# Router logits of an attention and expert block as four column-tiled products, with the expert choice moved later

## The reference

```
mod = silu(c) @ wmod                      # shifts, scales and gates a batch
h = layernorm(x) * (1 + ca) + sa
q = h @ W + b
w = exp(tanh((q @ h.T) * 1/|i - j|)), 0 on the diagonal
x = x + ga * (w @ h) / sum(w)
h2 = layernorm(x) * (1 + cb) + sb
logits = h2 @ Wg                          # 8 experts a token
top 2 of the 8, softmax over the two
x = x + gb * (sum over the two of weight * expert(h2) + shared(h2))
expert(h) = relu(h @ W1 + b1) @ W2 + b2, 128 -> 512 -> 128
```

## Time and profile before

| | us |
|---|---|
| median of 3 runs | 650.99 (649.42 to 651.34) |
| profiled execution, first to last instruction (its span) | 665.5 |
| TensorE busy in it | 618.6 (93%) |
| VectorE busy | 457.9 (69%) |
| ScalarE busy | 397.5 (60%) |
| POOL busy | 343.3 (52%) |

### The profile page before, as it was taken

The page is one execution under the profiler, slowest core; times in us unless marked ns, Lnnn a source line. Parts: engine busy times, 40 slices in busy tenths (PEclk is TensorE's granted clock), DMA queues, the critical chain, the costliest instruction groups (busy, mean ns, idle before and its releaser), DMA issues.

```text
span 665.5 us, 13395 instructions
## 1 busy us (share of the span) xinstructions
PE 618.6 (93%) x4311; PEld 560.6 (84%) x4311; DVE 457.9 (69%) x1415; ACT 397.5 (60%) x635; POOL 343.3 (52%) x341
## 2 busy tenths in 40 slices
PE   3898999999999998977898999999999999999995
PEld 3587988898889886866798999998989898898995
DVE  7889797989898969766666564544444454452698
ACT  3587887877878756524346556565555646463541
POOL 4541706757575765657460465655565656465100
PEclk9899999999999999887999999999999999999998
DMA  8030000111111111111165466656666665521692
GB/s 299 27 158 1 1 1 17 37 34 33 34 33 38 33 42 33 37 39 43 49 196 200 129 197 190 181 172 193 195 188 182 187 182 178 175 65 30 268 386 113
DMA packets 29884, 76.44 MB, mean 115 GB/s; under 512 B 7126, under 2 KB 11374, under 8 KB 29712
## 3 DMA queue, kind: packets, MB, share of 16 engines
q1 hardware_dynamic: 20480, 58.49, 27.2%
q0 software_dynamic: 8640, 16.93, 7.5%
q10 hardware_dynamic: 720, 0.47, 0.2%
HBM read 53.53 MB, written 23.24 MB: 115 GB/s over the span
## 4 chain that ended last, share of the span: by engine, by line
PE 33%; DVE 8%; issue 5%; another core or an unknown queue 2%; DMA 2%; POOL 2%; ACT 1%; SPq 0%; POOLq 0%; ACTq 0%; DVEq 0%
PE value L1940 12%; PE score L1733 5%; PE misc L1940 5%; PE score L1731 5%; PE score L1732 4%; PE value L1991 2%; POOL rows_x L576 2%; DVE h_hi L1271 1%; DMA h_t<-rows_z 1%; ACT work L967 1%; DVE tile_y L1560 1%; PE misc L1772 1%; DVE tile_y L1552 0%; DMA lw<-rows_x 0%
## 5 line engine op out<-in xcount | busy, mean ns | idle before, releaser
L780 POOL DMA_INDIRECT rows_z<-tile_y,tags x138 | 142.5, 1032 | 118.8 <-issue 37.5
L1731 PE MATMUL score<-h_hi,h_lo 128*128 128x512 f32 (+1 forms) x252 | 94.9, 376 | 3.9 <-DVE rows_all L1177 3.8
L1759 PE MATMUL value<-w_ring,work 128*128 128x129 f32 x768 | 93.8, 279 | 1.6 <-ACT work L840 1.0
L1759 PEld LDWEIGHTS value<-w_ring,work 128*128 128x128 f32 x768 | 91.2, 194 | 4.1 <-issue 1.6
L967 ACT ACTIVATE work<-score,w_ring 128x512 f32<-128x512 f32 (+1 forms) x96 | 53.2, 616 | 61.7 <-PE score L1733 44.5
L1733 PE MATMUL score<-h_hi,h_lo 128*128 128x512 f32 (+1 forms) x252 | 89.4, 355 | 0.0
L1732 PE MATMUL score<-h_hi,h_lo 128*128 128x512 f32 (+1 forms) x252 | 88.9, 353 | 0.0
L576 POOL DMA_INDIRECT rows_x<-work,slot x64 | 64.5, 1008 | 45.5 <-issue 16.3
L838 ACT ACTIVATE work<-work 128x1024 f32<-128x1024 f32 x64 | 67.2, 1050 | 27.2 <-DVE work L1168 22.1
L1168 DVE TENSOR_TENSOR work<-score,lw 128x1024 f32<-128x1024 f32 x64 | 76.6, 1216 | 2.7 <-PE score L1733 1.2
L967 ACT ACTIVATE work<-score,w_shared 128x512 f32<-128x512 f32 x64 | 39.9, 685 | 57.9 <-PE score L1733 45.6
(11 more groups left out here) (254 smaller groups left out, 1269.0 us busy)
## 6 DMA issues: line engine op xcount, KB each, us to landing
w_ring<-packs SPq DMA_DIRECT2D x24, 578.0 KB
rows_all<-packs SPq DMA_DIRECT2D x23, 578.0 KB
lw<-rows_x SPq DMA_DIRECT2D x24, 260.0 KB
res<-x SPq DMA_DIRECT2D x8, 512.0 KB, 6.3
h_t<-rows_z SPq DMA_DIRECT2D x3, 1024.0 KB, 11.0
mod<-mod_rows SPq DMA_DIRECT2D x1, 2560.0 KB, 10.1
rows_z<-tile_y,tags POOLq DMA_INDIRECT x142
rows_all<-rows_z SPq DMA_DIRECT2D x2, 1024.0 KB, 13.0
```

The costliest lines, as they stand in the source:

```text
L780: nc.gpsimd.indirect_dma_start(rows_z[:, :], bass.IndirectOffsetOnAxis(ap=tags[pos][:, k, 0:1].bitcast(I32), axis=0), tile_y[par][:, k, :] ...
L1731: nc.tensor.matmul(out, a_lo, b_hi, start=True, stop=False)
L1759: ins = nc.tensor.matmul(value[:, s // 3, c0:c0 + D + 1], prob[:, t % 4, s * P:(s + 1) * P], normal[b % 3][:, t, :], start=(t == 0 and s % ...
```

## The change

The weights of the router are padded from 8 to 32 columns with zeros, and the roles are swapped: they become the stationary side, and 256 tokens the moving side. Four such products (`gate_panes`) fill `misc`: pane j takes tokens 256j to 256j + 255 of the batch's order and writes partitions 32j to 32j + 31, that is, column tile j of TensorE's array. ScalarE copies the 128x256 result to `gate_t` (`stage_gate`), TensorE transposes it back in two pieces (`gate_logits`), and VectorE's `choose` copies the 8 of each 32 columns that count. In batches 2 to 7 the transposes, the choice and the count of batch b - 2 now stand in batch b instead of at the end of batch b - 1. `take_ranks` moves behind `scale_attended`, `ranks` behind `scores(b, 2)`.

```diff
-        wg_sb = sb("wg_sb", [D, E])
+        wg_sb = sb("wg_sb", [D, COL])
+        gate_t = sb("gate_t", [P, S // PANES])
...
+            nc.gpsimd.memset(wg_sb[:, E:COL], 0.0).then_inc(wg_cleared, 1)
             nc.gpsimd.iota(lw_from[:, :].rearrange("p (g q) -> p g q", q=P), pattern=[[1, G], [G, P]],
...
+            def stage_gate(b):
+                act.wait_ge(gate_ps_ready, b + 1)
+                nc.scalar.activation(gate_t[:, :], misc[:, 0:S // PANES], ACT.Copy).then_inc(gate_staged, 1)
...
             def last_batch(b):
-                gap_exponent(b - 2)
+                stage_gate(b - 2)
                 weights(b, 0)
                 weights(b, 1)
+                gap_exponent(b - 2)
...
                 weights(b, 6)
+                stage_gate(b - 1)
                 weights(b, 7)
...
                     return last_batch(b)
+                stage_gate(b - 2)
                 transposed(b + 1, 1 - par, 0)
...
             stage_h2t(B - 1, 1, xt_ps)
+            stage_gate(B - 1)
             split_x(3, 1, shared_rows(3))
...
-                nc.vector.tensor_copy(logits[:, :, :].rearrange("p g e -> p (g e)"), misc[:, 0:G * E]).then_inc(logits_ready, 1)
+                gates = misc[:, S // PANES:2 * (S // PANES)].rearrange("p (t j e) -> p t j e", j=PANES, e=COL)
+                nc.vector.tensor_copy(logits[:, :, :].rearrange("p (j t) e -> p t j e", j=PANES), gates[:, :, :, 0:E]).then_inc(logits_ready, 1)
...
-                if exists(b - 2):
-                    count_chosen(b - 2, route_chain[b - 2])
                 weigh(b, 0)
+                route_chain[b - 2] = choose(b - 2)
                 weigh(b, 1)
+                count_chosen(b - 2, route_chain[b - 2])
                 attend(b - 1)
-                if exists(b - 2):
-                    take_ranks(b - 2)
                 scale_attended(b - 1)
+                take_ranks(b - 2)
                 weigh(b, 2)
...
-                route_chain[b - 1] = choose(b - 1)
...
+            def gate_panes(b):
+                pe.wait_ge(h2t_staged, 2 * b + 2)
+                if b == 0:
+                    pe.wait_ge(wg_cleared, 1)
+                for j in range(PANES):
+                    at = b * S + j * (S // PANES)
+                    ins = nc.tensor.matmul(misc[j * COL:(j + 1) * COL, 0:S // PANES], wg_sb[:, :], h2_t[:, at:at + S // PANES], start=True, stop=True)
+                ins.then_inc(gate_ps_ready, 1)
+
             def gate_logits(b):
-                pe.wait_ge(h2t_staged, 2 * b + 2)
-                for g in range(G):
-                    ins = nc.tensor.matmul(misc[:, g * E:(g + 1) * E], h2_t[:, b * S + g * P:b * S + (g + 1) * P], wg_sb[:, :], start=True, stop=True)
+                pe.wait_ge(gate_staged, b + 1)
+                for t in range(S // PANES // P):
+                    ins = nc.tensor.transpose(misc[:, S // PANES + t * P:S // PANES + (t + 1) * P], gate_t[:, t * P:(t + 1) * P], ident[:, :])
                 ins.then_inc(logits_ps_ready, 1)
...
                 scores(b, par, 0)
+                gate_logits(b - 2)
                 scores(b, par, 1)
                 pe.wait_ge(qt_ready, 2 * b + 2)
                 transpose_h(b + 1, 0)
                 values(b - 1, 1 - par, 6)
                 values(b - 1, 1 - par, 7)
-                if exists(b - 2):
-                    pe.wait_ge(ht_ready, 2 * b + 3)
-                    ranks(b - 2)
                 scores(b, par, 2)
+                pe.wait_ge(ht_ready, 2 * b + 3)
+                ranks(b - 2)
                 transpose_h(b + 1, 1)
...
-                gate_logits(b - 1)
+                gate_panes(b - 1)
...
             transpose_h2(B - 1, 1, xt_ps, last_xhat)
+            gate_panes(B - 1)
             gate_logits(B - 1)
```

More of the change, by code:

```diff
@@ L61 @@
 FRONT = 8
+PANES = 4
+COL = P // PANES
 RING = 3
@@ L310, in adaln_moe @@
         h2t_staged = sem("h2t_staged")
+        wg_cleared = sem("wg_cleared")
+        gate_ps_ready = sem("gate_ps_ready")
+        gate_staged = sem("gate_staged")
         logits_ps_ready = sem("logits_ps_ready")
@@ L803, in _ @@
             act.dma_start(batt_sb[:, :], b_att).then_inc(small_loaded, 16)
-            act.dma_start(wg_sb[:, :], wg).then_inc(small_loaded, 16)
+            act.dma_start(wg_sb[:, 0:E], wg).then_inc(small_loaded, 16)
             def modulation():
@@ L1310, in last_batch @@
             def last_batch(b):
+                weigh(b, 0)
+                route_chain[b - 2] = choose(b - 2)
+                attend(b - 1)
+                weigh(b, 1)
                 count_chosen(b - 2, route_chain[b - 2])
-                weigh(b, 0)
-                attend(b - 1)
+                weigh(b, 2)
                 take_ranks(b - 2)
-                weigh(b, 1)
-                weigh(b, 2)
                 weigh(b, 3)
@@ L1805, in last_batch @@
                 scores(b, par, 0)
+                gate_logits(b - 2)
                 values(b - 1, 1 - par, 7)
                 scores(b, par, 1)
+                scores(b, par, 2)
                 ranks(b - 2)
-                scores(b, par, 2)
                 scores(b, par, 3)
```

## The result

The changed kernel takes **686.76 us** (median of 6 runs, 684.90 to 691.48), the kernel before 651.16 beside it: ratio 1.055, 95% interval 1.053 to 1.057, so +35.6 us. The profiled execution of the change is itself the longest of its six: its mean granted clock is 0.953, that of the other five 0.960 to 0.970, so it holds more of the clock's loss than the median does. That of the kernel before, shown above, is 14.5 us over its median.

The account below looks back on a forecast made before the run. It took TensorE to bound batches 2 to 6. Stops and added work +24 us, clock +7, batch 7 +0.5, last logits +0.8 and memset +0.2 made +32.5, carried to the 651 us median: 683 us, range 665 to 695.

Parts of the forecast that it names:

- The wait for ScalarE: TensorE, before the gate transposes in batches 2 to 6: stands still 2.5 us for ScalarE's queued copy.
- the rival's 3.8: Same place, if the panes run side by side: TensorE stands still 3.8 us, transposes starting at the same time.
- The wait for the ranks: TensorE, before transpose_h(b + 1, 1): stops 2.8 us until VectorE's later take_ranks, where there was 0.3.
- The clock: Behind the ten new stops in batches 2 to 6: half are followed by low clock, +7 us (0 to +17).
- VectorE's order: VectorE in the batches: the choice moved later frees it where it only waited, 0 us.
- The sum of five batches: Batches 2 to 6: +24 us from +4.8 per batch, plus 7 for the clock.
- Batch 7: Batch 7: no stop for ScalarE, ranks wait for a later count; 0 to +1, taken as +0.5 us.
- The last logits: End of the attention stage: +0.8 us with panes one after the other, or -1.5 side by side.
- panes side by side: Rival: TensorE saves 1.0 us per batch, gaining only in batch 7 and the tail; 680 us, chance 0.15.
- Only one stop costs: Rival: ScalarE's lag shrinks, so the first stop goes and the second stays; 666 us, chance 0.10.
- Faster: Rival: copy finds ScalarE free (lag under 3.2 us), ranks read in time, panes parallel; 640 us, chance 0.05.

Follow-up runs that it names:

- e1: The changed kernel with ScalarE's copy of the panes moved ahead of weights(b, 6): 676.0 us, 1.038 of the kernel before.
- The fillers: The run e4: dummy products that nothing waits for keep TensorE busy in both stops of the changed kernel; 678.2 us.
- e4: The changed kernel with dummy products filling TensorE's two stops, nothing waiting for them: 678.2 us, 1.042 of the kernel before.
- e3: The changed kernel with both edits, the copy ahead of weights(b, 6) and take_ranks directly behind attend: 664.1 us, 1.022 of the kernel before.
- the second trace of before: The kernel before, unchanged, profiled once more: span 649.4 us, batches 2 to 6 in 160.6 us.
- e7: The kernel of e6 with four more panes a batch, all eight's extra four written to one column tile: 662.1 us, 1.017 of the kernel before.
- e5: The changed kernel's new order with the eight products of before, no copy and no transposes: 680.4 us, 1.046 of the kernel before.
- e6: The changed kernel's panes, copy and transposes with, as near as possible, the order of before on every engine: 649.9 us, 0.9992 of the kernel before.
- e2: The changed kernel with take_ranks back directly behind attend, ahead of scale_attended: 673.2 us, 1.034 of the kernel before.
- e11: The same text as e6, run again on another chip: 678.3 us, 1.016 of the kernel before, which took 667.0 us there.

## Why the prediction was right, and where it was off

683 us was forecast, 686.8 measured. Step by step, from one batch's logits to the query product of the next (batch 3):

| stretch | before (first trace) | forecast | measured |
|---|---|---|---|
| logits to gate transposes | - | 5.74 | 5.80 |
| to the scores behind the values | - | 5.65 | 7.20 |
| to `transpose_h(b + 1, 1)` | - | 4.55 | 4.59 |
| to the query product | - | 3.8 | 6.47 |
| together | 14.94 | 19.7 | 24.06 |

- **The wait for ScalarE** ended where it was forecast (panes + 5.74), since ScalarE's queue sets it. Its length was 3.56 us, not 2.5: the panes run side by side, so TensorE arrives earlier, which the prediction had as the rival's 3.8 at the same end. In batch 2 it was 2.80. The copy took 0.37 (taken 0.45).
- **The wait for the ranks:** 2.62 us, five times (taken 2.8), and the old 0.50 us at the query product is gone, both as the text had it. In e1 it grew to 3.49 us when the choice moved ahead.
- **The clock** is the mis-sized term: "If half of ten fall", 1.7 us each, taken as +7. Nine of ten fell. The table holds 1.6 us of slow rows behind the first stop and 2.7 behind the second; by the same rows it is 2.6, 4.2, 4.3, 2.7 and 4.1 us in batches 2 to 6, together 18 us. The fillers gave back 12 us of them between the traces and 8.5 us in the plain runs, whose clock was higher than the traced one's. So half of the falls had been left out, and two things that the sum did not have worked against that: a part of the first fall lies under VectorE's chain, and some of the time comes back as other waits. By the plain runs +7 was near.
- **VectorE's order** was put at nothing ("The choice moved later frees VectorE at a place where it only waited: 0"). With a full clock, in e4, the way from the gate transposes to the second stop's end took 10.1, 11.6, 11.0, 10.7 and 10.7 us, where the forecast had 10.2: choice and count now stand between `weigh(b, 0)` and `attend`, and in e1 and e3 the ranks wait 1.8 to 1.95 us for the count in batches 3 to 6.
- **The sum of five batches** was 24 + 7; measured 39.7, and 27.3 with the fillers. **Batch 7**, taken +0.5, measured +2.6: the ranks wait 2.65 us for the later count there, where the second trace of before has 0.23, and the clock falls behind that wait (0.50 from 293.5 to 297.5 us); I had put the wait at 1 at most, without following VectorE's order.
- **The last logits**, taken +0.8 (serial) or -1.5 (side by side), measured 2.76 us to VectorE's read instead of 3.62, -0.86: the panes are side by side (1.08 us at the low clock), but VectorE read the logits 0.5 us late, behind its own residual work. All that follows the last logits' start is 1.3 us shorter, so nothing of it was lost.
- **The nearness of the number is in part luck:** +32 was forecast, the plain runs have +35.6 and the traces +40.3. The five batches were 8.7 us too low and batch 7 2.1, the last logits and what follows were too high, and the plain runs have a higher mean clock than the traced one.
- **The rivals:** panes side by side is what happened (e7), with the small effect given it, since a wait for ScalarE swallowed it. "Only one stop costs" fell: five and five were there. "Faster" named a lag under 3.2 us as its point; it was 5.5 in batch 3 (119.72 to 125.20).
- **Which part costs what:** the new order alone +29.4 us (e5), the panes alone 0 on that chip (e6), both +35.6. That the order is most of it, even without the copy, the prediction did not see: it named the place of the copy and of `take_ranks`, but not that the choice and the count, put behind `weigh(b, 0)` and `weigh(b, 1)`, are late for the ranks (1.9 us in e1 and e3).

## What to carry to other kernels

Where one engine has 98% of a stretch, look up the lag of every other engine against it before giving it something to wait for: a small copy costs what is queued ahead of it, not its own 0.4 us. A saving on that engine is worth only what the next chain leaves: in e6 the products and transposes were 0.9 us a batch cheaper, TensorE was busy 0.55 us less, and 0.5 us of that became a longer wait at the query product. And a short stop has a second price, the slow rows behind it, which was as large as the stop behind the second one here (2.7 us beside 2.62).

## What was not expected of the hardware

- Four f32 products with 32 columns of weights, in four column tiles, took 0.57 us together; in one tile 1.72 us. The eight products of before, with 128 columns of weights and 8 moving, took 1.70 us.
- A stop of 2.81 us was followed by the low clock and one of 3.24 us was not (e2); the five of 2.60 to 2.62 us all were (the changed kernel).
- Multiplying by zeros kept the granted clock at 1.00: in the fillers the moving side is a zero column.
- One kernel had no measurable difference to its neighbour on one chip (0.9992) and cost 1.6% on another (e6 and e11), a chip that itself ran the kernel before 1.5 to 2.5% slower. A margin under 2% from one chip is worth a second one.
